# Sum of sines: PSUM slots used strictly in turn with three fills ahead, and the weights divided by the head's largest

## The chip, the cores and the metric

The kernel runs on one core of a Trainium2 chip. The metric is the device time of one execution in microseconds (us); lower is better. Of TensorE (PE), VectorE (DVE), ScalarE (ACT), GpSimd (POOL) and SyncE (SP, which here only issues DMAs) each has its own stream of instructions, and they meet at semaphores.

## The reference, cut to what matters

```python
B, L, D, H, hd = 8, 1024, 256, 16, 16
FREQS = [31.0, 37.0, 41.0, 43.0, 47.0]
sim = einsum('bhid,bhjd->bhij', q, k) / sqrt(hd) / (abs(temperature)[0] + 0.1)
scores = 0
for fi, freq in enumerate(FREQS):
    scores = scores + alpha[:, fi] * sin(TWO_PI * sim / freq + phi[:, fi])
w = sigmoid(scores)
w = w / (sum(w, axis=-1) + 1e-10)
out = einsum('bhij,bhjd->bhid', w, v)
```

In front of it stand the projections q, k and v; behind it the output projection, layer norms, and a second block in which a router picks 127 of each 1024 tokens for a small attention and a feed-forward layer. The change touches none of that second block. For every batch and head (8 x 16 = 128 of them) a 1024 x 1024 matrix of angles is needed five times, once for each frequency.

## The kernel before

The kernel has three stages, one after the other.

**project_qkv** (0 to about 407 us) computes q, k and v for eight batches. DVE scales q by one over each of the five frequencies and splits each product into a rounded part and a rest (`split_q`, L246 and L250), and SP writes them to HBM (`q_d`), 80 transfers of 1 MB. Before its first batch DVE works out the temperature (L225 to L233) and copies the turned weights out of PSUM (L236); PE's first turn of x (L187) waits for that copy and for the load of x.

**oscillatory_attention** (about 407 to 6800 us) goes over 128 heads. A head is cut into eight units of 128 keys by 1024 queries; n numbers the units from 0 to 1023. For a unit:

- PE fills a PSUM slot with the angle of one frequency, in turns and with whole turns taken off (`fill`, L465: eight matmuls, in four pairs; the two of a pair go to the two halves of the slot). There are three slots of two banks, `ps_turn[0..2]`.
- ACT takes the sine of the slot into `wave` (L537), five times a unit, and once a unit the tanh of the finished sum of the unit before (L531), between its fourth and fifth sine.
- DVE multiplies the first sine by its weight (L586) and adds the four others with theirs (L562, four times). The weights stand in `head_c`, one value for each frequency, the same on all partitions. POOL copies them there for each head (L444).
- Every second unit PE multiplies two finished weight tiles by v (`times_v`, L485). Once a head DVE copies the product out (L580), and SP stores it.

The slots are given by hand, as `SLOT = [0, 1, 2, 0, 1]`: frequency 1 and frequency 4 of a unit share slot 1, and slot 2 serves frequency 2 alone. `FILLED_AT = [2, 3, 1, 4, 5]` says after which count of fills each frequency may be read: PE fills the next unit's frequency 2 first (after this unit's third sine), then 0 (after the fourth), then 1 (after the fifth). So frequency 1 of the next unit can be filled only when the fifth sine of this one has ended. In the order of a unit that is, with s0 to s4 for the sines and T for the tanh: s0, s1, s2, s3, T, s4, and on PE: 3, 4, next 2, next 0, (times_v), next 1.

DVE may start a unit's sum as soon as s0 is there. ACT may be two units ahead of DVE (`wait_pos(act, summed, n - 1)`).

SP loads q, k and v of the next head while the present one is worked on. All engines go over the heads with `heads_of`: four heads written out, 61 turns of a loop of two heads, and the last ones written out.

Ahead of the first head SP loads alpha and phi (L369, L371), DVE reduces the phases in seven small steps and spreads them over rows (L557), POOL clears the tiles, SP writes fixed rows and the phase rows (L383), and then loads the first head.

**routed_block** (about 6800 us to the end) is the rest.

Of the kernel before, what the change touches and what calls it, by code (L numbers as in the profile page):

```python
# [22 lines left out]
H, HD = 16, 16  # L23
# [22 lines left out]
ONE_ROW = 3 * HD + 2  # L46
TURN_IN = -TWO_PI * (1.0 - 2.0 ** -19)
# [27 lines left out]
def project_qkv(nc, x, wq, bq, wk, bk, wv, bv, temperature, q_d, k_d, v_d, vs_d):  # L75

    with ExitStack() as ctx:
# [7 lines left out]
        temp = sb("p_temp", [P, 5])  # L85
        x_in = sb("p_x_in", [P, 2, LT, D])
# [18 lines left out]
        q_step, q_split, k_step, k_split = sem("q_step"), sem("q_split"), sem("k_step"), sem("k_split")  # L105
        totals, tot_ready, tot_kept = sem("totals"), sem("tot_ready"), sem("tot_kept")

        with nc.Block() as block:

            @block.sync  # L110
            def _(sp):
                for n, w in enumerate((wq, wk, wv)):
                    sp.dma_start(w_in[:, n, :, :], w.rearrange("(m p) i -> p m i", p=P)).then_inc(w_loaded, 16)
# [105 lines left out]
            def _(dve):  # L219
# [3 lines left out]

                dve.wait_ge(b_loaded, 80)
# [28 lines left out]
                with dve.Fori(0, B, 1) as b:  # L253
# [8 lines left out]
                    dve.wait_ge(q_ready, b + 1)  # L262
                    split_q(b, 0)
# [43 lines left out]
def oscillatory_attention(nc, alpha, phi, q_d, k_d, v_d, ph_d, o_d):  # L307
# [3 lines left out]
    with ExitStack() as ctx:  # L311
# [4 lines left out]
        phase = sb("a_phase", [HF, 5])  # L316
        phase_hl = sb("a_phase_hl", [HF, 2])
# [34 lines left out]

        LOADS = 16 * 14
# [7 lines left out]
        SLOT = [0, 1, 2, 0, 1]  # L361
        FILLED_AT = [2, 3, 1, 4, 5]
        halved = lambda half: slice(half * HALF, (half + 1) * HALF)

        with nc.Block() as block:

            @block.sync
            def _(sp):
                sp.dma_start(table[:].rearrange("p h f -> p (h f)"),  # L369
                             alpha.rearrange("h f -> (h f)").partition_broadcast(P)).then_inc(table_in, 16)  # L370
                sp.dma_start(phase[:, 0:1], phi.rearrange("h (f o) -> (h f) o", o=1),  # L371
                             allow_slow_non_contiguous=True).then_inc(table_in, 16)
# [9 lines left out]
                sp.wait_ge(phase_step, 9)  # L382
# [39 lines left out]
            def _(pool):  # L422
# [16 lines left out]
                pool.wait_ge(table_in, 32)  # L439

                def constants(g, k):

                    wait_pos(pool, summed, (g - 1) * U)
# [11 lines left out]
            def _(pe):  # L455
                def fill(n, s, k, f):
# [6 lines left out]
                    for i, w in enumerate(weights):  # L463
                        for half in range(2):
                            last = nc.tensor.matmul(ps_turn[SLOT[f]][:, half, :], exact(w(rows[half])), exact(q_r[rows[half], k, f, :]),  # L465
# [3 lines left out]
                def fill_next(n, s, k, i):  # L469

                    if not unit_in(n + 1):
                        return
                    if s < U - 1:
                        fill(n + 1, s + 1, k, i)
                    else:
                        fill(n + 1, 0, 1 - k, i)
# [15 lines left out]
                fill(0, 0, 0, 2)  # L492
                fill(0, 0, 0, 0)
                fill(0, 0, 0, 1)

                def body(g, k):
                    for s in range(U):
                        n = g * U + s
                        if main(g):
                            pe.wait_ge(sines, NF * n + 1)  # L500
                            fill(n, s, k, 3)
                            pe.wait_ge(sines, NF * n + 2)
                            fill(n, s, k, 4)
# [739 lines left out]
```

## Time and profile before

| | |
|---|---|
| time, median of 3 runs (lowest, highest) | 7689.26 us (7687.89, 7692.23) |
| the profiled execution: its time | 7687.41 us |
| its span, first to last instruction | 7685.7 us |
| busy: PE, DVE, ACT, POOL | 6453.2, 6887.9, 5960.5, 155.8 us |
| busy share: PE, DVE, ACT, POOL | 84%, 90%, 78%, 2% |
| mean granted TensorE clock (1 is full speed) | 0.945 |

The span is read in stretches: three stages with different limits stand behind the shares of busy time. More than four fifths of the span is the attention stage, in which the same unit of work is repeated 1024 times, so that a tenth of a microsecond in a unit is 102 us of time. "Idle before" names how long an engine stood still just before a group of instructions, and what it waited for. An ACTIVATE or a DVE operation can start before the one ahead of it has ended, so the distance from start to start is what counts, not the duration.

### The profile page before, as it was taken

The numbers are of one execution on the slowest core, as the hardware profiler recorded it, in microseconds if no ns is written. First come the engines' busy times: TensorE is split into PE (matmuls) and PEld (weight loads), VectorE is DVE, ScalarE is ACT, GpSimd is POOL, SyncE is SP. The second block draws the span as 40 slices with busy tenths as digits, with TensorE's granted clock in tenths as the row PEclk, the third lists the DMA queues.
The fourth block names the chain that finished last, engine by engine and source line by source line (L and its number), as shares of the span: only waits on it lengthen the run. The fifth ranks groups of instructions, "written<-read, shape, count | busy, mean of one in ns | idle before, by whom it ended". The sixth has DMA issues, their size and how long they took to land. (4 is left out here: it accounts for less than half of the span.)

```text
span 7685.7 us, 139488 instructions
## 1 busy us (share of the span) xinstructions
PE 6453.2 (84%) x48057; PEld 4156.2 (54%) x48057; DVE 6887.9 (90%) x7386; ACT 5960.5 (78%) x6386; POOL 155.8 (2%) x217
## 2 busy tenths in 40 slices
PE   6459999999999999999999999999999999945555
PEld 3335555555555555555555555555555555524444
DVE  5659999999999999999999999999999999957776
ACT  1059999999999999999999999999999999931112
POOL 0000000000000000000000000000000000000000
PEclk8779999999999999999999999999999999976666
DMA  7821111111111111111111111111111111121120
GB/s 304 353 84 40 42 42 42 41 41 40 41 40 40 41 42 42 42 41 41 40 40 40 40 41 42 42 41 41 41 40 40 40 40 42 42 58 51 52 52 19
DMA packets 320072, 438.72 MB, mean 57 GB/s; under 512 B 156596, under 2 KB 187220, under 8 KB 319000
## 3 DMA queue, kind: packets, MB, share of 16 engines
q1 hardware_dynamic: 314648, 432.80, 17.7%
q0 software_dynamic: 5376, 5.30, 0.3%
q8 instruction: 28, 0.46, 0.0%
q14 instruction: 20, 0.16, 0.0%
HBM read 284.10 MB, written 153.75 MB: 57 GB/s over the span
## 5 line engine op out<-in xcount | busy, mean ns | idle before, releaser
L562 DVE SCALAR_TENSOR_TENSOR a_weight<-a_wave,a_head_c,a_weight 128x1024 f32<-128x1024 f32 x4096 | 5263.0, 1285 | 296.6 <-ACT a_wave L537 127.5
L537 ACT ACTIVATE a_wave<-a_ps_turn 128x1024 f32<-128x1024 f32 x5120 | 4926.4, 1033 | 597.1 <-PE a_ps_turn L465 597.1
L465 PE MATMUL a_ps_turn<-a_q_r,a_k_r 64*128 64x512 f32 x20480 | 3771.5, 413 | 632.1 <-ACT a_wave L537 529.2
L465 PE MATMUL a_ps_turn<-a_q_r,a_rounder 64*128 64x512 f32 x20480 | 3205.5, 390 | 0.0
L465 PEld LDWEIGHTS a_ps_turn<-a_q_r,a_k_r 64*128 64x128 f32 x20480 | 1920.2, 184 | 2347.9 <-ACT a_wave L537 1776.8
L465 PEld LDWEIGHTS a_ps_turn<-a_q_r,a_rounder 64*128 64x128 f32 x20480 | 1932.7, 185 | 249.6
L531 ACT ACTIVATE a_weight<-a_weight 128x1024 f32<-128x1024 f32 x1024 | 1097.0, 1071 | 7.5 <-DVE a_weight L562 6.1
L586 DVE TENSOR_SCALAR a_weight<-a_wave,a_head_c 128x1024 f32<-128x1024 f32 x1024 | 765.5, 748 | 55.8 <-ACT a_wave L537 55.8
L485 PE MATMUL a_ps_out<-a_weight,a_v_r 128*32 128x512 f32 x4096 | 546.4, 605 | 7.0 <-ACT a_weight L531 6.4
L444 POOL COPY a_head_c<-a_table 128x5 f32 (+1 forms) x128 | 64.3, 503 | 6203.3 <-DVE a_weight L562 6203.2
L485 PEld LDWEIGHTS a_ps_out<-a_weight,a_v_r 128*32 128x32 f32 x4096 | 80.7, 108 | 193.3 <-ACT a_weight L531 140.3
L301 ACT ACTIVATE p_qk_sb<-p_lo,p_bias 128x1024 f32<-128x1024 f32 x16 | 16.9, 1110 | 215.6 <-DVE p_k_hl L280 200.0
L206 PE MATMUL p_hi<-p_w_t,p_x_t 128*128 128x256 f32 x256 | 71.8, 449 | 107.6 <-DVE p_qk_sb L256 107.6
L246 DVE TENSOR_SCALAR p_q_hl<-p_qk_sb 128x1024 fp32r<-128x1024 f32 x80 | 52.5, 689 | 118.6 <-DMA q_d<-p_q_hl 118.6
L879 PE MATMUL Bk<-ident,logits 128*127 128x128 f32 x128 | 30.3, 431 | 117.9 <-ACT logits L927 117.9
L206 PEld LDWEIGHTS p_hi<-p_w_t,p_x_t 128*128 128x128 f32 x256 | 58.4, 232 | 124.2 <-DVE p_qk_sb L256 113.4
L927 ACT ACTIVATE spread<-spread 128x8 f32<-128x8 f32 x24 | 5.0, 209 | 134.1 <-DVE spread L1014 134.0
L820 PE MATMUL A<-woa_t,o_t 128*128 128x256 f32 x256 | 69.6, 433 | 27.8 <-DVE o_t L1043 27.8
L879 PEld LDWEIGHTS Bk<-ident,logits 128*127 128x127 f32 x128 | 27.9, 334 | 120.1 <-ACT logits L927 120.1
L198 PE MATMUL p_hi<-p_x_t,p_w_t 128*128 128x512 f32 x128 | 69.9, 708 | 27.0 <-ACT p_x_t L295 27.0
L250 DVE SCALAR_TENSOR_TENSOR p_q_hl<-p_qk_sb,p_q_hl 128x1024 fp32r<-128x1024 f32 x80 | 92.1, 1218 | 0.0
L580 DVE COPY a_out<-a_ps_out 128x512 f32<-128x512 f32 x128 | 87.5, 684 | 3.2 <-PE a_ps_out L485 3.2
(212 smaller groups left out, 1904.2 us busy)
## 6 DMA issues: line engine op xcount, KB each, us to landing
q_d<-p_q_hl SPq DMA_DIRECT2D x80, 1024.0 KB, 8.5
a_q_r<-q_d SPq DMA_DIRECT2D x256, 320.0 KB
a_k_r<-k_d SPq DMA_DIRECT2D x512, 128.0 KB
a_q_r<-q_d SPq DMA_DIRECT2D x256, 160.0 KB
k_d<-p_k_hl SPq DMA_DIRECT2D x8, 4096.0 KB, 15.5
a_k_r<-k_d SPq DMA_DIRECT2D x512, 64.0 KB
o_d<-a_out SPq DMA_DIRECT2D x512, 34.0 KB
num<-o_d SPq DMA_DIRECT2D x32, 512.0 KB
```

What stands on the lines that cost most here:

```text
L198: last = nc.tensor.matmul(out[:, 2 * m + half, :], w_t[:, n, c, m * P:(m + 1) * P], x_t[:, c, half * HALF:(half + 1) * HALF], start=(c == ...
L206: last = nc.tensor.matmul(hi[:, t // 2, (t % 2) * D:(t % 2 + 1) * D], x_t[:, c, t * P:(t + 1) * P], w_t[:, 2, c, :], start=(c == 0), stop= ...
L250: nc.vector.scalar_tensor_tensor(q_hl[:, f, 1, :].bitcast(F32R), whole, 1.0 / FREQS[f], q_hl[:, f, 0, :], ALU.mult, ALU.subtract).then_inc ...
L444: nc.gpsimd.tensor_copy(head_c[:, k, :], table[:, bass.ds(g % H, 1), :].rearrange("p h f -> p (h f)")).then_inc(const_ready, 1)
L465: last = nc.tensor.matmul(ps_turn[SLOT[f]][:, half, :], exact(w(rows[half])), exact(q_r[rows[half], k, f, :]), start=(i == 0), stop=(i == 3))
L485: last = nc.tensor.matmul(ps_out[VP * c:VP * (c + 1), :], v_r[:, k, t + c // 2, :], weight[:, (t + c // 2) % RING, halved(c % 2)], start=( ...
L531: nc.scalar.activation(tile, tile, ACT.Tanh, scale=0.5).then_inc(squashed, 1)
L537: nc.scalar.activation(wave[:, s % 2, f, :], ps_turn[SLOT[f]][:].rearrange("p a b -> p (a b)"), ACT.Sin, scale=TURN_IN).then_inc(sines, 1)
L562: return v.scalar_tensor_tensor(weight[:, s % RING, :], wave[:, s % 2, f, :], head_c[:, k, f:f + 1], weight[:, s % RING, :], ALU.mult, ALU ...
L580: v.tensor_copy(out[:, 1 - k, :], ps_out[:]).then_inc(out_ready, 1)
L586: v.tensor_scalar(weight[:, s % RING, :], wave[:, s % 2, 0, :], head_c[:, k, 0:1], None, ALU.mult).then_inc(added, 1)
L820: ins = mm(A[:, 2 + t // 2, (t % 2) * D:(t % 2 + 1) * D], o_t[:, c, half * HALF + t * P:half * HALF + (t + 1) * P], woa_t[:, c, :], start= ...
```

## The change

The angle's slots are used strictly in turn: fill number m (5 n + f) goes to slot m modulo 3, and PE fills three ahead of the sine that it waits for. As 40 fills a head is not a multiple of 3, the slot of a fill depends on the head modulo 3, and for PE and ACT the loop is unrolled over six heads (`heads_in_turn`). The other engines keep the loop of two.

The weights of a head are divided by the one with the largest magnitude, and that one's frequency is put first. So the first sine needs no multiplication: the first add takes `wave[0]` as it is, and L586 is gone. The tanh's scale, 0.5 before, is now half of that largest weight, read from `head_c`, one value for each partition. As the frequencies now stand in an order that depends on the head, `split_q` takes one over the frequency from a table (`rate`), one value for each partition. The table, with the weights and the phases, is made in 46 small steps by DVE at the start of project_qkv, on tiles of 16 partitions and up to 5 elements, written to HBM and read back; attention loads its weights and phases from there.

```diff
 def project_qkv(...):
             def _(sp):
+                sp.dma_start(tab[:, 0, :], alpha).then_inc(tab_in, 16)
+                sp.dma_start(tab[:, 2, :], phi).then_inc(tab_in, 16)
                 for n, w in enumerate((wq, wk, wv)):
...
                 load(0, 0)
                 load(1, 1)
+                sp.wait_ge(tab_done, 1)
+                sp.dma_start(tab_d, tab[:]).then_inc(tab_kept, 16)
+                sp.wait_ge(tab_kept, 16)
+                for m in range(KC):
+                    sp.dma_start(rate[:, m, :], tab_d[8 * m:8 * m + 8, 1, :].unsqueeze(1).broadcast_to([8, HD, NF])).then_inc(rate_in, 16)
...
             def _(dve):
+                tabs = Chain(dve, tab_step, 0, TAB_STEPS, 0)
+                step = tabs.step
+                for f in range(NF):
+                    step(v.memset(tab[:, 1, f:f + 1], 1.0 / FREQS[f]))
+                dve.wait_ge(tab_in, 32)
...
+                v.tensor_tensor(tab[:, 3, :].bitcast(F32R), work[0], tab[:, 2, :], ALU.subtract).then_inc(tab_done, 1)
 
                 dve.wait_ge(b_loaded, 80)
...
-                        nc.vector.tensor_scalar(q_hl[:, f, 0, :].bitcast(F32R), whole, 1.0 / FREQS[f], None,
+                        nc.vector.tensor_scalar(q_hl[:, f, 0, :].bitcast(F32R), whole, rate[:, m, f:f + 1], None,
                                                 ALU.mult).then_inc(q_step, 1)
...
-                        nc.vector.scalar_tensor_tensor(q_hl[:, f, 1, :].bitcast(F32R), whole, 1.0 / FREQS[f],
+                        nc.vector.scalar_tensor_tensor(q_hl[:, f, 1, :].bitcast(F32R), whole, rate[:, m, f:f + 1],
...
 def oscillatory_attention(...):
+        def heads_in_turn(eng, body):
+            for g in range(8):
+                body(g, g % 2, g % 3)
+            with eng.Fori(1, HEADS // 6 - 1, 1) as six:
+                for j in range(2, 8):
+                    body(6 * six + j, j % 2, j % 3)
+            for g in range(HEADS // 6 * 6 - 4, HEADS + 1):
+                body(g, g % 2, g % 3)
...
-        SLOT = [0, 1, 2, 0, 1]
-        FILLED_AT = [2, 3, 1, 4, 5]
+        SLOTS = 3
+        slot_of = lambda r, s, f: (r * U * NF + s * NF + f) % SLOTS
...
-                sp.dma_start(table[:].rearrange("p h f -> p (h f)"),
-                             alpha.rearrange("h f -> (h f)").partition_broadcast(P)).then_inc(table_in, 16)
-                sp.dma_start(phase[:, 0:1], phi.rearrange("h (f o) -> (h f) o", o=1),
-                             allow_slow_non_contiguous=True).then_inc(table_in, 16)
+                sp.dma_start(table[:],
+                             tab_d[:, 0, :].partition_broadcast(P)).then_inc(table_in, 16)
+                for i in range(2):
+                    sp.dma_start(phase[:, i:i + 1], tab_d[:, 2 + i, :].rearrange("h (f o) -> h f o", o=1),
+                                 allow_slow_non_contiguous=True).then_inc(table_in, 16)
...
 POOL, constants:
-                    wait_pos(pool, summed, (g - 1) * U)
+                    wait_pos(pool, squashed, (g - 1) * U)
...
 PE:
-                fill(0, 0, 0, 2)
-                fill(0, 0, 0, 0)
-                fill(0, 0, 0, 1)
+                for f in range(SLOTS):
+                    fill(0, 0, 0, f)
...
+                        for f in range(NF):
+                            if main(g):
+                                pe.wait_ge(sines, NF * n + f + 1)
+                                if s == U - 1 and f == NF - SLOTS and unit_in(n + 1):
+                                    pe.wait_ge(qk_loaded[1 - k], loads_of(g + 1, 1 - k))
+                                fill_ahead(n, s, k, r, f)
+                            if f != NF - 2:
+                                continue
+                            if s % 2 and s >= 3 and main(g):
+                                times_v(n - 3, s - 3, g, k)
+                            if s == 1 and after(g):
+                                times_v(n - 3, U - 2, g - 1, 1 - k)
+                heads_in_turn(pe, body)
...
 ACT:
-                                nc.scalar.activation(tile, tile, ACT.Tanh, scale=0.5).then_inc(squashed, 1)
+                                nc.scalar.activation(tile, tile, ACT.Tanh, scale=head_c[:, k if s else 1 - k, 0:1]).then_inc(squashed, 1)
...
-                            act.wait_ge(filled, NF * n + FILLED_AT[f])
+                            act.wait_ge(filled, NF * n + f + 1)
...
 DVE: the seven phase steps are gone; the sum of a unit:
-                            dve.wait_ge(sines, NF * n + 1)
-                            v.tensor_scalar(weight[:, s % RING, :], wave[:, s % 2, 0, :], head_c[:, k, 0:1], None,
-                                            ALU.mult).then_inc(added, 1)
-                            for f in range(1, NF - 1):
-                                dve.wait_ge(sines, NF * n + f + 1)
-                                add_wave(n, s, k, f).then_inc(added, 1)
+                            dve.wait_ge(sines, NF * n + 2)
+                            add_wave(n, s, k, 1, wave[:, s % 2, 0, :])
+                            for f in range(2, NF - 1):
+                                more_wave(n, s, k, f)
```

## Rows read from the trace of the kernel before

**Rows 1.** Costliest groups: line, operation, count | busy us, mean ns | idle before, releaser.

```profile
L562 DVE SCALAR_TENSOR_TENSOR a_weight<-a_wave,a_head_c,a_weight 128x1024 f32<-128x1024 f32 x4096 | 5263.0, 1285 | 296.6 <-ACT a_wave L537 127.5
L537 ACT ACTIVATE a_wave<-a_ps_turn 128x1024 f32<-128x1024 f32 x5120 | 4926.4, 1033 | 597.1 <-PE a_ps_turn L465 597.1
...
L246 DVE TENSOR_SCALAR p_q_hl<-p_qk_sb 128x1024 fp32r<-128x1024 f32 x80 | 52.5, 689 | 118.6 <-DMA q_d<-p_q_hl 118.6
...
L250 DVE SCALAR_TENSOR_TENSOR p_q_hl<-p_qk_sb,p_q_hl 128x1024 fp32r<-128x1024 f32 x80 | 92.1, 1218 | 0.0
L580 DVE COPY a_out<-a_ps_out 128x512 f32<-128x512 f32 x128 | 87.5, 684 | 3.2 <-PE a_ps_out L485 3.2
```

**Rows 2.** One stretch: PE, PEld, DVE, ACT, POOL busy; granted clock; DMA share, GB/s.

```profile
3000.00:5000.00 2000.00, 1833.36 (x14282) 1151.17 (x14276) 1907.77 (x1665) 1826.37 (x1948) 20.16 (x40) 1.00 0.14 41
```

**Rows 3.** ACT in order of time: start us, length us, merged instructions, idle before.

```profile
3017.72 1.95 ACT L537 ACTIVATE a_wave<-a_ps_turn 128x1024 f32<-128x1024 f32 x2
3020.05 2.86 ACT L537 ACTIVATE a_wave<-a_ps_turn 128x1024 f32<-128x1024 f32 x3 [0.38 <-PE a_ps_turn L465]
3022.78 1.07 ACT L531 ACTIVATE a_weight<-a_weight 128x1024 f32<-128x1024 f32 x1
3023.73 1.95 ACT L537 ACTIVATE a_wave<-a_ps_turn 128x1024 f32<-128x1024 f32 x2
```

**Rows 4.** PE in order of time in the same units.

```profile
3018.81 0.50 PE L465 MATMUL a_ps_turn<-a_q_r,a_k_r 64*128 64x512 f32 x2 [0.63 <-ACT a_wave L537]
...
3021.93 0.63 PE L465 MATMUL a_ps_turn<-a_q_r,a_k_r 64*128 64x512 f32 x4
...
3022.86 0.62 PE L465 MATMUL a_ps_turn<-a_q_r,a_k_r 64*128 64x512 f32 x4
...
3024.09 1.07 PE L485 MATMUL a_ps_out<-a_weight,a_v_r 128*32 128x512 f32 x8
3025.08 0.50 PE L465 MATMUL a_ps_turn<-a_q_r,a_k_r 64*128 64x512 f32 x2
```

**Rows 5.** DVE in order of time in the same units.

```profile
3020.37 0.75 DVE L586 TENSOR_SCALAR a_weight<-a_wave,a_head_c 128x1024 f32<-128x1024 f32 x1
3021.21 5.25 DVE L562 SCALAR_TENSOR_TENSOR a_weight<-a_wave,a_head_c,a_weight 128x1024 f32<-128x1024 f32 x4
3026.37 0.75 DVE L586 TENSOR_SCALAR a_weight<-a_wave,a_head_c 128x1024 f32<-128x1024 f32 x1
```

**Rows 6.** DVE in order of time, in one of the heads written out ahead of the loop.

```profile
600.02 5.45 DVE L562 SCALAR_TENSOR_TENSOR a_weight<-a_wave,a_head_c,a_weight 128x1024 f32<-128x1024 f32 x4
```

**Rows 7.** POOL in order of time: its copy for each head, in the loop.

```profile
3038.93 0.50 POOL L444 COPY a_head_c<-a_table 128x5 f32 x1 [48.73 <-DVE a_weight L562]
3088.19 0.51 POOL L444 COPY a_head_c<-a_table 128x5 f32 x1 [48.76 <-DVE a_weight L562]
3137.53 0.51 POOL L444 COPY a_head_c<-a_table 128x5 f32 x1 [48.83 <-DVE a_weight L562]
```

**Rows 8.** ACT in order of time: an activation whose bias is a per-partition operand.

```profile
34.13 2.12 ACT L301 ACTIVATE p_qk_sb<-p_lo,p_bias 128x1024 f32<-128x1024 f32 x2 [15.66 <-PE p_lo L198]
```

**Rows 9.** ACT in order of time: the stage's first sine and the last unit's fifth.

```profile
471.67 1.02 ACT L537 ACTIVATE a_wave<-a_ps_turn 128x1024 f32<-128x1024 f32 x1 [54.13 <-PE a_ps_turn L465]
...
6783.91 1.00 ACT L537 ACTIVATE a_wave<-a_ps_turn 128x1024 f32<-128x1024 f32 x1
```

**Rows 10.** The start of the kernel in order of time.

```profile
8.38 0.16 DVE L225 SCALAR_TENSOR_TENSOR p_temp<-p_temp 128x1 f32<-128x1 f32 x1 [8.38 <-DMA p_temp<-in_L_attn_temperature]
...
9.10 1.75 DVE L236 COPY p_w_t<-p_lo 128x1536 f32<-128x1536 f32 x1
...
11.58 3.56 PE L187 MATMUL p_lo<-p_ident,p_x_in 128*128 128x128 f32 x16 [3.25 <-DMA p_x_in<-in_L_attn_x]
```

**Rows 11.** SP in order of time, ahead of the first head.

```profile
431.90 0.44 SPq L383 DMA_DIRECT2D ph_d<-a_phase_rows  x1
```

**Rows 12.** DMA issues: queue, count, KB each, median us from issue to landing.

```profile
a_v_r<-v_d SPq DMA_DIRECT2D x128, 64.0 KB, 10.3
```

More of the change, by code:

```diff
@@ L46 @@
 ONE_ROW = 3 * HD + 2
+TAB_STEPS = 45
+TINY = 1e-30
 TURN_IN = -TWO_PI * (1.0 - 2.0 ** -19)
@@ L72, in wait_pos, with project_qkv @@
         eng.wait_ge(sem, value)
-def project_qkv(nc, x, wq, bq, wk, bk, wv, bv, temperature, q_d, k_d, v_d, vs_d):
+def project_qkv(nc, x, wq, bq, wk, bk, wv, bv, temperature, alpha, phi, q_d, k_d, v_d, vs_d, tab_d):
     with ExitStack() as ctx:
@@ L222, in _ @@
                 dve.sem_inc(x_summed, 1)
+                v = nc.vector
+                size, top, first, other, kept = (tab_w[:, n, :] for n in range(5))
+                work = [tab_w[:, n, :] for n in range(5, 8)]
+                tabs = Chain(dve, tab_step, 0, TAB_STEPS, 0)
[3 more added lines that the diff above has]
+                dve.wait_ge(tab_in, 32)
+                step(v.scalar_tensor_tensor(size, tab[:, 0, :], -1.0, tab[:, 0, :], ALU.mult, ALU.max))
@@ new lines, in _ @@
+                step(v.tensor_reduce(top[:, 0:1], size, AX.X, ALU.max))
+                step(v.tensor_scalar(size, size, top[:, 0:1], None, ALU.is_equal))
+                step(v.tensor_copy(first[:, 0:1], size[:, 0:1]))
+                step(v.tensor_copy(kept, size))
+                for f in range(1, NF):
+                    step(v.tensor_tensor(first[:, f:f + 1], kept[:, f:f + 1], kept[:, f - 1:f], ALU.is_gt))
+                    step(v.tensor_tensor(kept[:, f:f + 1], kept[:, f:f + 1], kept[:, f - 1:f], ALU.max))
@@ new lines, in _ @@
+                step(v.tensor_scalar(other, first, -1.0, 1.0, ALU.mult, ALU.add))
+                for i in range(3):
+                    step(v.tensor_tensor(work[0], tab[:, i, :], first, ALU.mult))
+                    step(v.tensor_tensor(work[1], tab[:, i, :], other, ALU.mult))
+                    step(v.tensor_copy(work[2][:, 0:1], tab[:, i, 0:1]))
+                    step(v.tensor_reduce(tab[:, i, 0:1], work[0], AX.X, ALU.add))
+                    step(v.scalar_tensor_tensor(tab[:, i, 1:NF], first[:, 1:NF], work[2][:, 0:1], work[1][:, 1:NF], ALU.mult, ALU.add))
@@ new lines, in _ @@
+                step(v.tensor_scalar(top[:, 1:2], top[:, 0:1], TINY, None, ALU.is_lt))
+                step(v.tensor_tensor(top[:, 2:3], top[:, 1:2], tab[:, 0, 0:1], ALU.add))
+                step(v.reciprocal(top[:, 3:4], top[:, 2:3]))
+                step(v.tensor_scalar(tab[:, 0, 1:NF], tab[:, 0, 1:NF], top[:, 3:4], None, ALU.mult))
+                step(v.tensor_scalar(tab[:, 0, 0:1], tab[:, 0, 0:1], 0.5, None, ALU.mult))
+                step(v.tensor_scalar(work[0], tab[:, 2, :], 1.0 / TWO_PI, ROUND, ALU.mult, ALU.add))
@@ L304, in _, with oscillatory_attention @@
                     last.then_inc(k_ready, 1)
-def oscillatory_attention(nc, alpha, phi, q_d, k_d, v_d, ph_d, o_d):
+def oscillatory_attention(nc, tab_d, q_d, k_d, v_d, ph_d, o_d):
     U = LT
@@ L464, in fill, with fill_ahead @@
                         for half in range(2):
-                            last = nc.tensor.matmul(ps_turn[SLOT[f]][:, half, :], exact(w(rows[half])), exact(q_r[rows[half], k, f, :]),
+                            last = nc.tensor.matmul(ps_turn[slot_of(r, s, f)][:, half, :], exact(w(rows[half])), exact(q_r[rows[half], k, f, :]),
                                                     start=(i == 0), stop=(i == 3))
                     last.then_inc(filled, 1)
[L469 to L476, printed above, removed]
+                def fill_ahead(n, s, k, r, f):
+                    if f + SLOTS < NF:
+                        fill(s, k, r, f + SLOTS)
+                    elif s < U - 1:
+                        fill(s + 1, k, r, f + SLOTS - NF)
+                    elif unit_in(n + 1):
+                        fill(0, 1 - k, r + 1, f + SLOTS - NF)
                 def times_v(n, t, g, k):
```

85 lines of the change are left out of this document (34 added, 51 removed).

## The prediction

> **What bounds the kernel now.** I read three views: the groups by cost, the busy time by stretch, and then, because two engines look equally full, the order of time of two units. The attention stage repeats one unit; in a stretch of 2000 us from its middle TensorE's granted clock is 1.00, its level of 2.4 GHz [rows 2]. DVE is busy 95% of that stretch, PE 92%, ACT 91% [rows 2], so the shares alone name DVE. The groups say otherwise: ACT stood idle 597.1 us, all of it for a fill of PE's, and DVE, the fullest engine, still lost 127.5 us to sines that came late [rows 1]. Something goes round between ACT and PE.
>
> The order of time shows what. Back to back sines start 0.92 us apart (two last 1.95, one 1.03) [rows 1, 3]. s4 starts at 3017.72 and ends at 3018.75; at 3018.81 PE starts the fill of the next unit's frequency 1 into the same slot; at 3020.05 ACT starts that sine, 1.24 us after the fill began [rows 3, 4]. Between s4's end and that start ACT had only s0 to do and stood 0.38 us. The round is: s1 to T 2.73 (3020.05 to 3022.78), T to s4 0.95, s4 itself 1.03, hand-over 0.06, fill 1.24: 6.01 us. With a times_v between the fills the fill starts 0.32 us after s4's end instead of 0.06 (3025.08 against 3023.73 + 1.03) [rows 3, 4], so 6.27. Four units of each make 49.1 us; a head takes 49.26 and 49.34 [rows 7].
>
> DVE alone would need nearly as much: from L586 to L586 6.00 us, of which 5.16 are the four adds and 0.84 the multiplication [rows 5]; eight of these and the head's copy of 0.68 [rows 1] are 48.7 us. In the heads written out the adds are slower (5.45 for four against 5.25) [rows 5, 6], and DVE is the bound there. So two limits lie within 0.6 us of each other, and either edit alone would gain little; this change takes away both.
>
> **The change, part by part.** The stage's ends: first sine at 471.67, the last unit's s4 at 6783.91 [rows 9]. From s0 to s4 inside a unit are about 4.6 us, so 1023 units took 6307.6, or 6.166 each.
>
> *ACT after.* If no sine waits, a unit is four distances between sines of 0.914 (2.86 less 1.033, halved), s3 to T 0.90 (2.73 less 1.83), T to s4 0.95 [rows 3]: 5.51. The tanh now reads a per-partition scale. No tanh of before has one. Nearest row: two activations with a per-partition bias take 2.12 where two sines take 1.95 [rows 3, 8], 0.17 over two, 0.09 each (both read PSUM, so that is not the difference). From below: nothing, if the read is hidden behind the T's own longer time. I take 0.09: the row has the same kind of operand. ACT: 5.60 a unit, 44.8 a head.
>
> *DVE after.* L586 goes (0.84). The first add reads two tiles of `wave` instead of one and the sum, the same number of streams, so it costs an add. A unit is 5.16, with the copy 5.25; written out 0.20 more, 5.45. Both are under 5.60. ACT waits for DVE in two places: T for the fifth add of the unit before, which is over 1.3 us after that sine's end while T starts 3.5 after it, and s0 for a sum a whole unit old. Neither binds.
>
> *PE after.* A fill that follows another takes 0.93 (four pairs, 3021.93 to 3022.86), times_v 0.99, and the fill behind it starts anew with about 0.11 more [rows 4]. Two units: ten fills 9.3, one times_v 0.99, 0.11: 10.4, or 5.20 each, under 5.60. Is it also in time? Sine f+3 needs the slot that sine f leaves. It should start 2.74 after sine f's start, 1.71 after its end. A fill needs 1.24 from its start when PE waited, about 1.13 when it runs on. So PE may lag a sine's end by 0.47 to 0.58. In the unit with times_v (5.73 of work against ACT's 5.60) the lag is 0.17 behind s3, and by my count 0.15 behind s4 and 0.3 behind the next four sines, before the following unit (4.65 of work) clears it. It holds, with 0.2 in hand. The tanh itself gives PE a step without a fill.
>
> So ACT sets the pace: 1023 x (6.166 - 5.60) = **579 us gained**.
>
> The Trainium skill (Runtime: NRT & Kernel Launch, section Instruction fetch mechanics) says that a taken branch to a page that has not been fetched stalls the engine for the fetch. It gives no time for it. The trace bears on it: each loop turn of before is two heads, and the heads that hold the branch back differ from the others by 0.08 us at most (49.26 and 49.34) [rows 7], so 61 turns cost under 5 us, or are covered by the waits that now go. After, PE and ACT turn 19 times. I count 0 either way.
>
> *Start of project_qkv.* SP issues two DMAs first. DVE's 46 small steps stand ahead of the temperature steps and of the copy L236; four such steps, each waiting for the one before, stand between 8.38 and 9.10, so one takes 0.18 [rows 10]. alpha and phi should be there at about 4 us, an estimate (the temperature, the last of SP's eight first loads, is there at 8.38), with the five memsets before that; 41 x 0.18 = 7.4, then 0.7 for the temperature: L236 starts at 12.1 instead of 9.10 and ends at 13.9; PE's first turn of x moves from 11.58 to 13.9, **+2.3**. Everything behind it moves with it, since the stage is paced by its stores: DVE waits 118.6 us for them at L246 [rows 1]. Bounds: +1 (SP's two issues alone) and +6. The rate loads run under 18 us of projection before the first split. The split's scalars become per-partition: an add with one costs 1285, the split's with a constant 1218 ns [rows 1], 0.07 each. Most hides behind the transfers; what stands ahead of the next transfer is the last of the five products and the first rest, two of them for each of 16 splits: **+2**.
>
> *Start of attention.* The seven phase steps go. The weights' load is now 2048 pieces of 20 bytes. The nearest row is v's load of 1024 pieces of 64 bytes, 10.3 us to landing [rows 12]; doubled, the phases are here at about 428 and the rows (5 us of DVE) at 433, where SP would store them at 431.9 [rows 11]: **+1** (0 to +8). ACT's first sine needs one fill instead of two, but the third has to wait as before: **-1**.
>
> Nothing else moves: POOL's copy waits for another count, and has a head's time.
>
> Sum: -579 + 2.3 + 2 + 1 - 1 = -575. The profiled execution took 7687.4 (span 7685.7 and 1.7 around it), the median is 1.9 above it. 7689.3 less that (574.7 before rounding) is **7115 us**, 7.5% less.
>
> **The rivals.**
>
> *A, ACT sets the pace at 5.60* (76 in 100): above. Its own range is 7090 to 7150 (unit 5.58 to 5.63).
>
> *B, the per-partition scale is free* (10 in 100): 5.51 a unit, 92 us less, 7023.
> The Trainium skill (ScalarE: Activation LUTs, section What ACT_TABLE_LOAD costs) puts 93 ns on each such operand of an ACTIVATE. That is A's price to the nanosecond of the rows above, and speaks against B.
>
> *C, PE sets the pace* (9 in 100). The strict turn asks PE for one fill per sine with no slack but the tanh. If each fill has to start anew, as the one at 3018.81 did, it takes 1.03 (0.93 and about 0.10) and 0.06 of hand-over, 1.09. PE passes ACT's 5.60 when three of five fills are such. Four of five make 4.36 + 0.93 + half a times_v = 5.79, 7309 us; all five 5.95, 7115 + 1023 x 0.35 = 7473. I take 7309 as its time, since PE gets a respite behind the tanh. For it: times_v comes while the slots are due. Against it: in before, the fills behind the first one ran on at 0.93.
>
> *D, no gain* (2 in 100): the pace is held by something that is not changed, SP's loads of the next head for instance: within 15 us of 7689. Against it: the round through slot 1 adds up to the observed head within 0.2 us.
>
> *E, slower* (3 in 100): the loop of six heads cannot be fed. Place: PE's and ACT's return at the end of each of 19 turns. Price: a stop for the fetch that was hidden with two heads. It decides from 575 / 19 = 30 us a turn; at 40 us the time would be 7115 + 760 = 7875. Against it: PE took the heads written out at full pace, and the turns of before show no stop of even 0.1 us.
>
> **How the numbers follow.** Below 7010 lies nothing that I can name. B's 7023 is in. Above A's own range I go to 7210, which takes in a unit of 5.69, a mix of A and a little of C. That leaves out most of C, D and E, 14 in 100. Faster by over 0.2% (15 us, about what this measurement tells from no change): A, B and C, 0.95. D: 0.02. E: 0.03.
>
> **What would show it.** Right: ACT's distances 0.92, 0.90 and 1.04 with no idle in the loop, heads 44.8 us apart at POOL, DVE idle 0.35 a unit behind sines, PE idle about 0.4. The tanh at about 1150 ns. Wrong: ACT idle behind L465 in every second unit (C); a tanh of 1071 ns (B); head distances that jump every sixth head (E); a first turn of x later than 18 us.

## The result, and the profile after

| | before | after |
|---|---|---|
| median, us | 7688.58 (7686.77 to 7692.23, four runs) | 7224.85 (7220.47 to 7230.59, four runs) |
| ratio, 95% interval | | 0.9397 (0.938 to 0.9413) |
| profiled execution, its span, us | 7687.4, 7685.7 | 7230.6, 7228.8 |

The change gains 464 us, 6.0%. The forecast was 574 us and 7115, its range 7010 to 7210: the result lies outside, 15 us above it.

The page of after, from its parts 1 to 3 and 5:

```profile
PE 6221.3 (86%) x48057; PEld 4381.9 (61%) x48057; DVE 6206.7 (86%) x6401; ACT 5948.7 (82%) x6386; POOL 193.9 (3%) x217
...
q8 instruction: 422, 6.91, 0.4%
...
q14 instruction: 135, 1.10, 0.0%
...
L591 ACT ACTIVATE a_wave<-a_ps_turn 128x1024 f32<-128x1024 f32 x5120 | 4983.1, 1203 | 152.1 <-PE a_ps_turn L526 141.6
...
L605 DVE SCALAR_TENSOR_TENSOR a_weight<-a_wave,a_head_c 128x1024 f32<-128x1024 f32 x1024 | 1314.2, 1283 | 390.0 <-ACT a_wave L591 388.9
L585 ACT ACTIVATE a_weight<-a_weight,a_head_c 128x1024 f32<-128x1024 f32 x1024 | 1356.2, 1324 | 1.8 <-DVE a_weight L605 1.8
```

Against [rows 1], where ACT lost 597.1 us to PE's fills, it loses 141.6, and 52.9 of these are the wait ahead of the stage's first sine. The multiplication of L586 is gone, and DVE's first add of a unit (the form with two inputs) is what waits for sines, 390.0 us of waiting. Two lines that the prediction never looked at have grown: the queues that carry instructions. The same two on the page of before:

```profile
q8 instruction: 28, 0.46, 0.0%
q14 instruction: 20, 0.16, 0.0%
```

So PE of after fetches 394 packets, 6.5 MB, more of instructions (q8; the runs below show that q8 goes with PE's loop and q14 with ACT's), and ACT 115 packets more.

One unit of ACT's timeline in the middle of the stage (start, us, how many in a row), which answer to [rows 3]:

```profile
3002.46 1.31 ACT L585 ACTIVATE a_weight<-a_weight,a_head_c 128x1024 f32<-128x1024 f32 x1
3003.50 4.85 ACT L591 ACTIVATE a_wave<-a_ps_turn 128x1024 f32<-128x1024 f32 x5
3008.03 1.37 ACT L585 ACTIVATE a_weight<-a_weight,a_head_c 128x1024 f32<-128x1024 f32 x1
```

Tanh to tanh is 5.57 us, tanh to s4 1.04, and there is no idle in between: the steady state is the predicted one. The heads are not all alike, though. POOL's copies, one for each head [rows 7]:

```profile
2716.95 0.94 POOL L505 COPY a_head_c<-a_table 128x5 f32 x1 [43.93 <-ACT a_weight L585]
2764.17 0.22 POOL L505 COPY a_head_c<-a_table 128x5 f32 x1 [46.28 <-ACT a_weight L585]
2813.30 0.94 POOL L505 COPY a_head_c<-a_table 128x5 f32 x1 [48.91 <-ACT a_weight L585]
2858.16 0.94 POOL L505 COPY a_head_c<-a_table 128x5 f32 x1 [43.93 <-ACT a_weight L585]
...
2992.77 0.94 POOL L505 COPY a_head_c<-a_table 128x5 f32 x1 [43.92 <-ACT a_weight L585]
3041.36 0.21 POOL L505 COPY a_head_c<-a_table 128x5 f32 x1 [47.65 <-ACT a_weight L585]
```

Four distances of 44.87, then two long ones (here 47.22 and 49.13), every six heads: the point where the loop of six returns to its top. Over the whole stage 36 distances are long. The 125 distances exceed 125 x 44.87 by 111.2 us, and 19 turns have 18 returns: 6.2 us each. This is what a return does on ACT (the number in brackets is the idle time before the group):

```profile
2755.65 1.27 ACT L591 ACTIVATE a_wave<-a_ps_turn 128x1024 f32<-128x1024 f32 x1
2757.45 2.85 ACT L591 ACTIVATE a_wave<-a_ps_turn 128x1024 f32<-128x1024 f32 x3 [0.53 <-issue]
2761.91 1.02 ACT L591 ACTIVATE a_wave<-a_ps_turn 128x1024 f32<-128x1024 f32 x1 [1.60 <-PE a_ps_turn L526]
2762.83 1.14 ACT L585 ACTIVATE a_weight<-a_weight,a_head_c 128x1024 f32<-128x1024 f32 x1
2765.74 1.02 ACT L591 ACTIVATE a_wave<-a_ps_turn 128x1024 f32<-128x1024 f32 x1 [1.77 <-PE a_ps_turn L526]
2767.44 1.02 ACT L591 ACTIVATE a_wave<-a_ps_turn 128x1024 f32<-128x1024 f32 x1 [0.68 <-PE a_ps_turn L526]
2769.15 1.02 ACT L591 ACTIVATE a_wave<-a_ps_turn 128x1024 f32<-128x1024 f32 x1 [0.68 <-PE a_ps_turn L526]
2770.61 1.96 ACT L591 ACTIVATE a_wave<-a_ps_turn 128x1024 f32<-128x1024 f32 x2 [0.44 <-PE a_ps_turn L526]
```

and on PE:

```profile
2758.05 0.40 PE L526 MATMUL a_ps_turn<-a_q_r,a_k_r 64*128 64x512 f32 x2
2760.67 0.50 PE L526 MATMUL a_ps_turn<-a_q_r,a_k_r 64*128 64x512 f32 x2 [2.23 <-ACT a_wave L591]
...
2761.47 0.62 PE L526 MATMUL a_ps_turn<-a_q_r,a_k_r 64*128 64x512 f32 x4
2764.05 1.22 PE L526 MATMUL a_ps_turn<-a_q_r,a_rounder 64*128 64x512 f32 x4 [1.96 <-issue]
2764.86 1.26 PE L526 MATMUL a_ps_turn<-a_q_r,a_k_r 64*128 64x512 f32 x4
2765.72 1.26 PE L526 MATMUL a_ps_turn<-a_q_r,a_rounder 64*128 64x512 f32 x4
```

with the granted clock of these stretches (us; busy PE, PEld, DVE, ACT, POOL; granted clock; DMA share; GB/s):

```profile
2740.00:2757.00 17.00, 16.35 (x136) 11.06 (x136) 15.59 (x13) 16.92 (x19) 0.00 (x0) 1.00 0.07 18
2757.00:2762.00 5.00, 2.77 (x22) 1.73 (x19) 3.93 (x4) 2.95 (x4) 0.00 (x0) 1.00 0.19 61
2762.00:2767.00 5.00, 3.04 (x17) 2.94 (x16) 1.43 (x3) 2.99 (x3) 0.22 (x1) 0.63 0.28 77
2767.00:2772.00 5.00, 5.00 (x33) 5.00 (x32) 2.68 (x3) 3.43 (x4) 0.00 (x0) 0.68 0.16 58
```

At the pace of 0.914 a sine and 1.96 from s3 past the tanh to s4, ACT's starts show it step by step. s4 to s0 takes 1.80, 0.89 late: a stop of ACT's own, released by nothing but "issue". s0 to s3 takes 4.46, 1.72 late: PE stood 2.23 us. The releaser named there is a sine, but the sine that the fill needed, the new head's s0, had ended 2.2 us before (it starts at 2757.45 and a sine lasts 1.02, the fill starts at 2760.67), so it was PE's own return. s3 to s4 takes 3.83, 1.87 late: PE stood a second time, 1.96 us in the middle of a fill, for "issue". The next three distances are 0.79, 0.80 and 0.55 late: by then the granted clock had fallen to its level of 1.2 GHz for most of these microseconds, and half a fill (a line of four matmuls above) started every 0.85 us instead of every 0.46. Together 6.6 us, and POOL's two long distances are 6.6 above two of 44.87.

The ends of the stage: SP's store of the phase rows, and ACT's first sine [rows 9, 11]:

```profile
437.02 0.44 SPq L444 DMA_DIRECT2D ph_d<-a_phase_rows  x1
```

```profile
475.67 1.03 ACT L591 ACTIVATE a_wave<-a_ps_turn 128x1024 f32<-128x1024 f32 x1 [52.87 <-PE a_ps_turn L526]
```

The first sine is 4.0 us later than before (forecast 4.3).

### The profile page after: what moved, and what is told of

Same layout as the page of the kernel before. It is cut to its first block and busy times, and to the rows that moved or that the text cites. A ratio compares the mean times of both kernels' runs of the same rounds, so it can differ in the third digit from the quotient of the medians.

```text
span 7228.8 us, 135758 instructions
## 1 busy us (share of the span) xinstructions
PE 6221.3 (86%) x48057; PEld 4381.9 (61%) x48057; DVE 6206.7 (86%) x6401; ACT 5948.7 (82%) x6386; POOL 193.9 (3%) x217
## 5 line engine op out<-in xcount | busy, mean ns | idle before, releaser
L591 ACT ACTIVATE a_wave<-a_ps_turn 128x1024 f32<-128x1024 f32 x5120 | 4983.1, 1203 | 152.1 <-PE a_ps_turn L526 141.6
L605 DVE SCALAR_TENSOR_TENSOR a_weight<-a_wave,a_head_c,a_weight 128x1024 f32<-128x1024 f32 x3072 | 3947.1, 1285 | 193.2 <-ACT a_wave L591 73.6
L526 PE MATMUL a_ps_turn<-a_q_r,a_k_r 64*128 64x512 f32 x20480 | 3534.7, 404 | 377.3 <-ACT a_wave L591 262.8
L526 PE MATMUL a_ps_turn<-a_q_r,a_rounder 64*128 64x512 f32 x20480 | 3254.4, 393 | 29.2 <-issue 29.2
L526 PEld LDWEIGHTS a_ps_turn<-a_q_r,a_k_r 64*128 64x128 f32 x20480 | 1974.6, 186 | 1580.2 <-ACT a_wave L591 963.1
L526 PEld LDWEIGHTS a_ps_turn<-a_q_r,a_rounder 64*128 64x128 f32 x20480 | 1981.7, 186 | 332.6 <-issue 33.8
L605 DVE SCALAR_TENSOR_TENSOR a_weight<-a_wave,a_head_c 128x1024 f32<-128x1024 f32 x1024 | 1314.2, 1283 | 390.0 <-ACT a_wave L591 388.9
L585 ACT ACTIVATE a_weight<-a_weight,a_head_c 128x1024 f32<-128x1024 f32 x1024 | 1356.2, 1324 | 1.8 <-DVE a_weight L605 1.8
L296 DVE TENSOR_SCALAR p_q_hl<-p_qk_sb,p_rate 128x1024 fp32r<-128x1024 f32 x80 | 57.3, 750 | 112.3 <-DMA q_d<-p_q_hl 112.3
L921 PE MATMUL Bk<-ident,logits 128*127 128x128 f32 x128 | 30.2, 431 | 117.9 <-ACT logits L969 117.9
L300 DVE SCALAR_TENSOR_TENSOR p_q_hl<-p_qk_sb,p_rate,p_q_hl 128x1024 fp32r<-128x1024 f32 x80 | 97.0, 1278 | 0.0
```

What stands on the lines that cost most here:

```text
L526: last = nc.tensor.matmul(ps_turn[slot_of(r, s, f)][:, half, :], exact(w(rows[half])), exact(q_r[rows[half], k, f, :]), start=(i == 0), st ...
L585: nc.scalar.activation(tile, tile, ACT.Tanh, scale=head_c[:, k if s else 1 - k, 0:1]).then_inc(squashed, 1)
L591: nc.scalar.activation(wave[:, s % 2, f, :], ps_turn[slot_of(r, s, f)][:].rearrange("p a b -> p (a b)"), ACT.Sin, scale=TURN_IN).then_inc( ...
L605: v.scalar_tensor_tensor(weight[:, s % RING, :], wave[:, s % 2, f, :], head_c[:, k, f:f + 1], to, ALU.mult, ALU.add).then_inc(summed if f ...
```

## The experiments

Each kernel has four executions, with executions of the kernel before taken beside them. The median of before differs by up to 3.7 us from one such group to another (7686.81 to 7690.51), so kernels of different groups are compared by what each gains on the before of its own group. The question: is it the return of the long loop, or the strict turn of the slots (rival C, PE short of time), and does each of the other terms hold? A loop of six heads is what the strict turn asks for: a head's 40 fills leave three slots turned by one, so the slots repeat after three heads and slots and buffers after six. A loop of two heads needs slots that repeat within the loop; a table of five that repeats with each unit does that, and one exists that also frees the slots in time:

**e1_table.** The strict turn is replaced by a table that gives slot 2 to frequencies 2 and 4 and fills in the order 3, next 1, 4, next 0, next 2 (`REFILL`: for the sine that ended, how many units ahead and which frequency); PE and ACT go back to a loop of two heads. What else waits for a count of fills follows that order (SP's load of the next head, ACT's last fifth sine); the rest is as in after.

```diff
-        slot_of = lambda r, s, f: (r * U * NF + s * NF + f) % SLOTS
+        SLOT = [0, 1, 2, 0, 2]
+        FILLED_AT = [2, 2, 3, 4, 6]
+        REFILL = [(0, 3), (1, 1), (0, 4), (1, 0), (1, 2)]
...
+        def heads_by(eng, body, count):
+            first = count if count > 2 else 4
+            turns = (HEADS - 2 - first) // count
...
-                heads_in_turn(pe, body)
+                heads_by(pe, body, 2)
...
-                heads_in_turn(act, body)
+                heads_by(act, body, 2)
```

> The changed kernel with its weights, but the slots given by a table of five again, 0, 1, 2, 0, 2 for frequencies 0 to 4, so that every slot that comes back after two sines has the tanh between; PE and ACT return to the loop of two heads. Theory, that the returns of the loop of six cost 111 us (18 returns, 6.2 us each): the long heads go, all heads take about 44.9 us, about 7225 - 111 = 7114 us, and few instruction fetches (28 packets as in the kernel before). Rival, that the long heads come from the loads of the next head or from something else that recurs: they stay, about 7225. Rival, that the table does not hold off the wait between s4 and the next s1: above 7225.

7116.37 us (7113.57 to 7121.26), ratio 0.9256 (0.9241 to 0.9272). No head is longer than the others (POOL's copies):

```profile
2726.18 0.94 POOL L508 COPY a_head_c<-a_table 128x5 f32 x1 [43.93 <-ACT a_weight L589]
2771.05 0.94 POOL L508 COPY a_head_c<-a_table 128x5 f32 x1 [43.93 <-ACT a_weight L589]
```

and the instruction queue is back at 28 packets:

```profile
q8 instruction: 28, 0.46, 0.0%
```

It gains 570.4 us (before of its group: 7686.81) and is the fastest kernel with the whole computation: 107 us more than the change, and its median lies within 2 us of the forecast. It changes two things at once, so the next runs put one back at a time.

**e2_pe6 and e3_act6.** e1 with a loop of six heads on PE alone, and on ACT alone.

```diff
-                heads_by(pe, body, 2)
+                heads_by(pe, body, 6)
```

```diff
-                heads_by(act, body, 2)
+                heads_by(act, body, 6)
```

> The kernel with the table 0, 1, 2, 0, 2, with PE alone in a loop of six heads (20 returns at most), ACT in a loop of two. If PE's return is what costs: 7114 + about 115, so 7215 to 7235, with a stop of PE in two pieces at every sixth head and the granted clock down behind it. If it is ACT's return, or both are needed: about 7114.

> The kernel with the table, with ACT alone in a loop of six heads, PE in a loop of two. If PE's return is what costs: about 7114 to 7130 (ACT's own idle without a releaser was 0.4 to 0.5 us a return, some 10 us in all). If ACT's return is what costs: 7215 to 7235.

PE alone: 7188.78 us (7185.01 to 7191.73), 72.4 more than e1, 3.8 for each of 19 returns. ACT alone: 7141.93 (7140.22 to 7142.76), 25.6 more, 1.3 a return. Both are real costs with the slot table of e1, so the strict turn isn't needed for them; PE's is three times ACT's. The expectations had put nearly all of after's 6.2 us on PE: e2 came out 26 us below its range, e3 12 us above. The waits of ACT in e3 between 1000 and 6000 us (total, times, longest) have the return itself:

```profile
ACT a_wave L595 <- issue: 24.6, 19, 1.5
```

Each engine fetches for itself: q8 has 406 packets in e2 and 28 in e3, q14 20 and 137.

**e4_pe4.** Is there a size from which it costs? e1 with a loop of four heads on PE.

```diff
-                heads_by(pe, body, 2)
+                heads_by(pe, body, 4)
```

> The kernel with the table, with PE alone in a loop of four heads, 30 turns. If four heads of PE's code are already more than it keeps: each return costs as in the loop of six, 30 x 6 = 180 us, about 7290, slower than with six heads. If four are kept: about 7114. If the cost grows with the size of the body and not with the returns: between the two, about 7190.

7250.75 us (7249.0 to 7257.03), 134.4 more than e1: 4.6 for each of 29 returns. Four heads are already too long, and slower than six because there are more returns; the expected 7290 took 6 us for each. Its queue:

```profile
q8 instruction: 446, 7.31, 0.4%
```

**e6_both14.** Does the cost go by the return, or by what is fetched? e1 with loops of 14 heads on both, 7 returns.

```diff
-                heads_by(pe, body, 2)
+                heads_by(pe, body, 14)
...
-                heads_by(act, body, 2)
+                heads_by(act, body, 14)
```

> The kernel with the table, with PE and ACT both in loops of fourteen heads, 8 turns. If each return costs a fixed time whatever the size of the body (6.2 us with both engines): 7116 + 50 = about 7166. If the cost comes from streaming the code, and so goes with the instructions fetched: about 7116 + 98 = 7214, as with six heads.

7144.44 us (7141.07 to 7147.03), a gain of 543.2 and so 27.2 less than e1's: 3.9 a return. It fetches nearly as much as the loops of four and six (392 packets), about 52 a return against 14 in e4, for a price per return that is no higher. So the stream of instructions is hidden behind the work; what costs is the start of it at each return. The time is 22 us below the expected 7166, again because 6.2 us a return was too much. The same holds at the place of after's loop: e10 below, with turns of twelve heads, has 392 packets to after's 422, but 8 returns to 18, at the same price of 6.0 and 5.9 us each.

**e9_both6.** e1 with loops of six heads on both engines: does the sum of e2 and e3 reach the 6 us a return of after?

```diff
-                heads_by(pe, body, 2)
+                heads_by(pe, body, 6)
...
-                heads_by(act, body, 2)
+                heads_by(act, body, 6)
```

> The kernel with the table, PE and ACT both in loops of six heads, 20 turns. If the returns of the two engines cost one after the other: 7116 + 72 + 26 = 7214. If PE's stop hides ACT's: about 7189, as with PE alone. If the two make each other worse, as the 6.2 us a return of the changed kernel would have it: 7240.

7197.22 us (7190.17 to 7198.26), a gain of 493.0, 77.4 less than e1's: 4.1 a return, less than e2 and e3 together (5.1), as expected if PE's stop hides a part of ACT's, and less than after. At the return PE stops once and not a second time:

```profile
1289.49 0.40 PE L529 MATMUL a_ps_turn<-a_q_r,a_k_r 64*128 64x512 f32 x2
1292.10 0.50 PE L529 MATMUL a_ps_turn<-a_q_r,a_k_r 64*128 64x512 f32 x2 [2.21 <-ACT a_wave L595]
1292.43 0.69 PE L529 MATMUL a_ps_turn<-a_q_r,a_rounder 64*128 64x512 f32 x4
1292.89 1.08 PE L529 MATMUL a_ps_turn<-a_q_r,a_k_r 64*128 64x512 f32 x4
```

That left two readings of the remaining 1.8 us: the strict turn, which has less slack, or the place of the code (e9's loop begins at head 6, after's at head 8). The last three runs cross them.

**e11_from6, e12_table_from8, e10_turn12.** e11 is after with its loop begun at head 6, with the same 19 turns of six. e12 is e9's kernel with its loop begun at head 8, 19 turns. e10 is after with turns of twelve heads from head 8.

```diff
-            for g in range(8):
+            for g in range(6):
...
-                for j in range(2, 8):
+                for j in range(6):
...
-            for g in range(HEADS // 6 * 6 - 4, HEADS + 1):
+            for g in range(HEADS // 6 * 6 - 6, HEADS + 1):
```

```diff
+        def heads_from8(eng, body):
+            for g in range(8):
+                body(g, g % 2)
+            with eng.Fori(1, HEADS // 6 - 1, 1) as six:
+                for j in range(2, 8):
+                    body(6 * six + j, j % 2)
...
```

```diff
-            with eng.Fori(1, HEADS // 6 - 1, 1) as six:
-                for j in range(2, 8):
+            with eng.Fori(1, 10, 1) as dozen:
+                for j in range(-4, 8):
...
-            for g in range(HEADS // 6 * 6 - 4, HEADS + 1):
+            for g in range(116, HEADS + 1):
```

> The changed kernel with its slots strictly in turn, with PE and ACT in a loop of twelve heads instead of six, 9 turns. If a return costs a fixed 6.2 us with the strict turn: 8 or 9 of them instead of 18, about 7225 - 60 = 7165. If a return costs 3.5 us as with fourteen heads and the table: about 7145. If the cost goes with the instructions fetched and not with the returns: 7225.

> The changed kernel, slots strictly in turn and the same number of turns of six heads, with the loop starting at head 6 instead of head 8, so that its code lies elsewhere. If the second stop of PE's, in the middle of a fill (2 us, and seen with the strict turn only), comes from where the code of the loop lies: a return costs about 4.2 us, 7116 + 76 = 7192. If it comes from the strict turn: 6 us, 7225 as before.

> The kernel with the table 0, 1, 2, 0, 2, PE and ACT both in the loop of six heads of the changed kernel, from head 8 with 19 turns, instead of from head 6 with 20. If the place of the code matters: about 7116 + 108 = 7224. If the strict turn matters: 4.2 us a return, about 7192.

| kernel | slots | loop | returns | median, us | gain | less than e1's | a return |
|---|---|---|---|---|---|---|---|
| e11_from6 | strict turn | 6, from head 6 | 18 | 7181.12 (7179.53 to 7181.87) | 509.4 | 61.0 | 3.4 |
| e9_both6 | table | 6, from head 6 | 19 | 7197.22 (7190.17 to 7198.26) | 493.0 | 77.4 | 4.1 |
| after | strict turn | 6, from head 8 | 18 | 7224.85 (7220.47 to 7230.59) | 463.7 | 106.7 | 5.9 |
| e12_table_from8 | table | 6, from head 8 | 18 | 7236.7 (7234.88 to 7238.46) | 453.8 | 116.6 | 6.5 |
| e10_turn12 | strict turn | 12, from head 8 | 8 | 7167.74 (7167.02 to 7169.22) | 522.4 | 48.0 | 6.0 |

Both came out on the side of the place, e11 11 us below the time expected for it and e12 13 us above. The strict turn has no price of its own: at either place it is a little cheaper than the table. The place has: from head 8 a return costs 5.9 to 6.5, from head 6 3.4 to 4.1. (For the strict turn e1 stands in as the kernel without returns. Its heads are 44.9 us and the steady ones of after 44.87.) The second stop goes with the place too. A return in e11, and one in e12 (PE):

```profile
1290.80 0.50 PE L526 MATMUL a_ps_turn<-a_q_r,a_k_r 64*128 64x512 f32 x2 [2.61 <-issue]
1291.13 0.94 PE L526 MATMUL a_ps_turn<-a_q_r,a_rounder 64*128 64x512 f32 x4
```

```profile
2760.52 0.50 PE L539 MATMUL a_ps_turn<-a_q_r,a_k_r 64*128 64x512 f32 x2 [2.73 <-ACT a_wave L605]
...
2764.11 1.22 PE L539 MATMUL a_ps_turn<-a_q_r,a_rounder 64*128 64x512 f32 x4 [1.59 <-issue]
```

The first stop, of 2.1 to 3.0 us, is at every return of PE, whether the profile puts it down to "issue" or to a sine. The second, of 0.4 to 2.2 us in the middle of a fill, is from head 8 at all 18 returns of after, 17 of 18 of e12 and all 8 of e10, and from head 6 at none (e2, e9, e11). From head 14 (e6) it is at none either, from head 4 (e4) at some. What is left between the two ways of using the slots, 0.6 to 0.7 us a return, lies where ACT differs: at a return its own stop is 0.7 us at most with the strict turn (after, e11) and, but for one return, 1.2 to 1.5 with the table (e9, e12). Why wasn't looked into.

What the lower clock costs can be read from returns of one run. Over the 10 us behind PE's stop the granted clock was 0.83 to 0.86 at most returns of e9, e11 and e2, and 1.00 at two, two and one of them; in after, with its second stop, it was 0.53 to 0.69 at 17 of 18. One of each kind, from e9 (start and end, us; busy PE, PEld, DVE, ACT, POOL; granted clock; DMA share; GB/s):

```profile
1292.10:1302.10 10.00, 9.81 (x68) 7.65 (x70) 7.02 (x6) 7.76 (x9) 0.21 (x1) 0.83 0.24 71
2656.58:2666.58 10.00, 9.70 (x80) 6.69 (x80) 8.47 (x7) 9.12 (x11) 0.22 (x1) 1.00 0.23 70
```

By POOL's distances a return at 1.00 cost 2.3 to 2.7 us, in all three runs, and the others 3.9 (e9, e2) and 3.5 (e11) on the mean: 0.9 to 1.4 us for the clock, with PE's stop itself alike. This is a comparison of returns, not an experiment.

**e5_tanh_const.** The other side of the steady pace: e1 with a constant scale of the tanh. It leaves out the multiplication of the sum by the head's largest weight.

```diff
-                                nc.scalar.activation(tile, tile, ACT.Tanh, scale=head_c[:, k if s else 1 - k, 0:1])
+                                nc.scalar.activation(tile, tile, ACT.Tanh, scale=0.5)
```

> The kernel with the table, with the tanh's scale a constant 0.5 again instead of the value for each partition; so the sum of sines is not multiplied by the head's largest weight. If the operand costs the 0.09 us a unit that I took: heads of 44.1 instead of 44.9 us, 7116 - 92 = about 7024. If it is free: 7116.

7030.16 us (7029.93 to 7032.14), a gain of 657.5, 87.0 more than e1's: 0.085 us for each of 1024 tanhs. The tanh to the next sine takes 0.94 to 0.95 again (ACT):

```profile
3002.98 1.11 ACT L589 ACTIVATE a_weight<-a_weight 128x1024 f32<-128x1024 f32 x1
3003.92 4.75 ACT L595 ACTIVATE a_wave<-a_ps_turn 128x1024 f32<-128x1024 f32 x5
```

That 87 us come back when one ACT instruction gets shorter also shows that ACT sets the pace.

**e7_slots_only and e8_weights_only.** Were both edits needed? e7 is the kernel before with e1's slot table and its order of fills, and nothing else. e8 is e1 with the slots and the order of fills of before, so with divided weights alone.

```diff
-        SLOT = [0, 1, 2, 0, 1]
-        FILLED_AT = [2, 3, 1, 4, 5]
+        SLOT = [0, 1, 2, 0, 2]
+        FILLED_AT = [2, 2, 3, 4, 6]
```

```diff
-        SLOT = [0, 1, 2, 0, 2]
-        FILLED_AT = [2, 2, 3, 4, 6]
-        REFILL = [(0, 3), (1, 1), (0, 4), (1, 0), (1, 2)]
+        SLOT = [0, 1, 2, 0, 1]
+        FILLED_AT = [2, 3, 1, 4, 5]
+        REFILL = [(0, 3), (0, 4), (1, 2), (1, 0), (1, 1)]
```

> The kernel before with the slot table 0, 1, 2, 0, 2 alone, and its multiplication of the first sine kept. Theory, that two limits lie close together: the round through slot 1 goes, DVE sets the pace at 6.00 us a unit, heads take 48.2 instead of 49.3 us (as three heads behind the written-out ones did in the kernel before): 7689 - 125 x 1.1 = about 7550. Rival, that the slots were all of the limit: heads of 44.9, about 7120. Rival, that they were no limit: 7689.

> The changed kernel with its divided weights, but the slots and the order of fills of the kernel before, 0, 1, 2, 0, 1, loops of two heads. Theory: the round through slot 1 stays and is longer by what the tanh's scale costs, 0.09 us a unit: heads of 50.0 us, DVE idle the rest: 7689 + 122 x 0.7 + 4 = about 7780, slower than before. Rival, that DVE was the limit: about 7120 to 7200.

e7: 7551.9 us (7550.75 to 7552.59), ratio 0.9824 (0.9808 to 0.984), 136 us faster than before; its heads are 48.2. Now it is DVE's sum that ACT waits for:

```profile
3004.49 1.06 ACT L531 ACTIVATE a_weight<-a_weight 128x1024 f32<-128x1024 f32 x1 [0.90 <-DVE a_weight L562]
```

e8: 7731.93 us (7730.49 to 7733.75), ratio 1.0058 (1.0041 to 1.0075), 44 us slower than before; its heads are 49.6. The old round through slot 1 is all there, and DVE merely waits longer; the tanh's scale makes the round longer by what it costs. ACT, and then DVE:

```profile
3003.90 2.86 ACT L595 ACTIVATE a_wave<-a_ps_turn 128x1024 f32<-128x1024 f32 x3 [0.38 <-PE a_ps_turn L529]
3006.63 1.17 ACT L589 ACTIVATE a_weight<-a_weight,a_head_c 128x1024 f32<-128x1024 f32 x1
3007.67 1.94 ACT L595 ACTIVATE a_wave<-a_ps_turn 128x1024 f32<-128x1024 f32 x2
```

```profile
3004.96 1.28 DVE L609 SCALAR_TENSOR_TENSOR a_weight<-a_wave,a_head_c 128x1024 f32<-128x1024 f32 x1 [0.86 <-ACT a_wave L595]
```

The expectation of e8 was 48 us too high: the loop's heads grew by 0.3 us where 0.7 was expected, and the heads written out became shorter (50.4 to 49.6), because DVE had bound them. Alone the edits are worth -136 and +44 us, together, with a loop of two, -570.

## Why the prediction was wrong, point by point

- **What bounds the kernel** (the round through slot 1 at 6.01 and 6.27 us, and DVE close behind it): right, but DVE was 1.1 us a head behind, not 0.6. e7 takes away the first and lands on the second (48.2 a head, predicted 48.7 for DVE); e8 takes away the second and stays on the first. "Either edit alone would gain little": 136 us gained and 44 lost.
- **ACT sets the pace at 5.60 a unit** (rival A's steady state): right. 44.87 a head is 5.609 a unit, 9 us more over the stage.
- **The tanh's scale at 0.09 us**: right, 0.085 measured (87 us in e5), and rival B is out. The Trainium skill (ScalarE: Activation LUTs, What ACT_TABLE_LOAD costs) has 93 ns; the run gives a little less. The prediction called that the rows' price "to the nanosecond", which it wasn't: 0.17 over two is 85 ns. The sign that I named for it, a tanh of about 1150 ns, was the wrong sign: the page has 1324. The distance to the next sine, 1.04, is the sign that held.
- **PE in time, with 0.2 us in hand** (rival C): right. Between 1000 and 6000 us ACT waits for fills 71 times, 88.4 us in all, and all 71 lie at the returns. (The unit with times_v adds up to 5.75 in the prediction's own terms, not 5.73, which changes nothing.)
- **Start of project_qkv, +2.3**: PE's first turn of x came at 13.48, +1.9. **Start of attention** as a whole: the first sine at +4.0 where +4.3 was the sum.
- **The step that failed: "61 turns cost under 5 us, or are covered by the waits that now go. After, PE and ACT turn 19 times. I count 0 either way."** The number for before was right, and it said nothing of after: a loop of two heads isn't fetched again (28 packets for the whole program), one of six is (422). The mechanism was in the prediction as rival E, but with a price from which it would turn the sign, 30 us a turn, and no bound below that in the sum or in the range. It costs 6 us a return. The sign named for E, head distances that jump every sixth head, is what the trace of after shows. On the profiled execution the forecast was 7687.4 - 574.7 = 7112.7, and 7230.6 was measured, 117.9 more: 111.2 of returns (18 x 6.2, from POOL's distances), 9 of the unit, and 2 us less for all the rest.
- The evidence offered against E, "PE took the heads written out at full pace", was of another thing: code that runs straight on, which e6 shows to be hidden in loops as well. Only the return stands.

The Trainium skill (Runtime: NRT & Kernel Launch, Instruction fetch mechanics) names the mechanism, a stall when a branch is taken to a page that isn't there. The runs agree: PE stops for 2.1 to 3.0 us at each return of a long loop, ACT for up to 1.5 us, and only the queue of the engine whose loop is long carries more packets.

**What stays open.** Why the place of the loop decides on the second stop wasn't found; only that it does, with both ways of using the slots. Whether a loop of three heads would still be kept wasn't tried. How much of a return's price is the lower clock is read from returns (2.1 of 6.6 us at one of after's; 0.9 to 1.4 where PE stops once), not from an experiment.

## What to carry to other kernels

A loop body that is made longer to get a rotation right can outgrow what the engine keeps of its code; then each return costs microseconds (here 3.8 to 4.6 on PE and 1.3 on ACT), so look at the instruction queues' packets before and after, and make the pattern fit a short body (here another slot table did, for 107 us more). If the long body must stay, make it much longer: the price goes by the number of returns. Where two limits lie close together, neither edit shows its worth alone: time them together before one is dropped.

## What the runs showed of the hardware that was not expected

- A loop of two heads on PE and ACT is not fetched again (28 packets on q8 and 20 on q14 for the whole program); PE's loops of 4, 6, 12 and 14 heads bring 392 to 446 packets on q8, 6.4 to 7.3 MB, whatever their length.
- A return of PE costs 3.8 to 4.6 us (e2, e4), one of ACT 1.3 (e3), both together 3.4 to 6.5, depending on where the loop lies (3.4 to 4.1 from head 6, 3.9 from head 14, 5.9 to 6.5 from head 8) and not on how much it fetches.
- A stop of PE of 2.1 to 3.0 us was mostly followed by a lower granted clock (0.83 over the next 10 us in e9, 0.66 in after with its second stop), but not always: in e11 one of 2.58 us had 1.00 behind it. Where the clock falls, the stall costs more than its own length.
- With ACT never waiting, its instructions last longer without starting further apart: sines 1203 ns on the mean where one alone lasts 1.02 us, at an unchanged distance of 0.92. Durations of a full engine don't give its pace; distances do. Why they grow wasn't looked into.
